# The maxima of the next head group spread over eleven slots of sixteen, and the long run of values three slots later

## The reference

```python
query = seq2 + b_self
key = concat([seq1 + b_prev, seq2 + b_self]); value = concat([seq1, seq2])
q, k, v = query @ Wq + bq, key @ Wk + bk, value @ Wv + bv      # split into 16 heads
score_prev = (q @ k_prev.T) * SCALE                            # masked past seq_len1
score_self = (q * k_self).sum(-1) * SCALE
weights = softmax(concat([score_prev, score_self]))
attn = weights[:-1] @ v_prev + weights[-1] * v_self
x = x + attn @ Wo + bo
h = gelu(x @ W1 + b1)
x = x + concat([h @ W2 + b2, h @ We[index] + be[index]])
```

## Time and profile before

| | |
|---|---|
| median of 3 runs | 1813.7 us (1807.92 to 1817.87) |
| profiled execution | 1807.68 us, span 1805.6 us |
| mean granted clock of TensorE | 0.975 of 2.4 GHz |
| busy | TensorE 1725.9 us (96%), weight loads 1266.5, VectorE 930.9, ScalarE 711.6, GpSimd 666.0 |
| first part | 32 groups, tiles of scores from 73.8 to 1005.7 us |
| length of a group in the middle | 25.2 to 38.2 us |

### The profile page before, as it was taken

One profiled execution on the slowest core, in us unless ns is written; L12 is line 12 of the kernel. 1 busy time (PEld: TensorE's weight loads), 2 busy tenths in 40 slices (PEclk: granted clock), 3 DMA queues, 4 the chain that ended last, 5 costly groups with the idle time before them and its releaser, 6 DMA issues.

```text
span 1805.6 us, 27964 instructions
## 1 busy us (share of the span) xinstructions
PE 1725.9 (96%) x8256; PEld 1266.5 (70%) x8256; DVE 930.9 (52%) x1430; ACT 711.6 (39%) x1259; POOL 666.0 (37%) x521
## 2 busy tenths in 40 slices
PE   6999999999999999999997899999999999999996
PEld 5666666657566566665662688888888888888885
DVE  4576576775766768657678633232232323232321
ACT  3254353544444435445445443323232323233322
POOL 3176575675774847657656301000010101010101
PEclk8999999999999999999997999999999999999998
DMA  6452435433534445253435432223141413232212
GB/s 143 76 115 62 108 80 115 92 77 82 111 93 88 92 88 117 52 109 83 97 82 150 115 115 50 68 49 85 46 87 41 87 52 78 59 66 70 47 30 53
DMA packets 370269, 149.45 MB, mean 83 GB/s; under 512 B 289226, under 2 KB 329162, under 8 KB 370194
## 3 DMA queue, kind: packets, MB, share of 16 engines
q1 hardware_dynamic: 364966, 146.28, 35.8%
q10 hardware_dynamic: 5228, 2.35, 0.5%
HBM read 70.41 MB, written 27.28 MB: 54 GB/s over the span
## 4 chain that ended last, share of the span: by engine, by line
PE 79%; issue 5%; DMA 4%; SPq 4%; DVE 4%; POOL 3%; ACT 1%; ACTq 0%; DVEq 0%; POOLq 0%
PE ps_proj L1258 15%; PE ps_av L1210 6%; PE ps_av L1212 6%; PE ps_av L1211 6%; PE ps_max L1289 6%; PE ps_av L1329 6%; PE ps_score L1316 5%; PE ps_proj L1210 3%; PE ps_proj L1211 3%; PE ps_proj L1212 3%; PE ps_max L1212 3%; PE ps_max L1211 3%; PE ps_max L1210 3%; DMA stacks<-parts 3%; PE ps_score L1212 3%
## 5 line engine op out<-in xcount | busy, mean ns | idle before, releaser
L729 ACT ACTIVATE p_f<-ps_score 128x512 f32<-128x512 f32 x512 | 304.0, 599 | 456.6 <-PE ps_score L1316 419.3
L941 DVE TENSOR_REDUCE m_col<-ps_max 128x1 f32<-128x512 f32 x512 | 328.7, 683 | 195.7 <-PE ps_max L1289 194.6
L604 POOL TENSOR_TENSOR p_sum<-p_sum,p_f 128x512 f32<-128x512 f32 x256 | 338.2, 1353 | 3.3 <-ACT p_f L729 3.3
L644 POOL TENSOR_TENSOR z_f<-z_f,a_raw 128x512 f32<-128x512 f32 x32 | 40.9, 1288 | 750.3 <-ACT z_f L842 726.0
L1135 DVE TENSOR_TENSOR h_lo<-h_f,h_hi 128x512 fp32r<-128x512 f32 x128 | 88.0, 688 | 411.8 <-ACT h_hi L833 411.7
L601 POOL TENSOR_TENSOR p_sum<-p_f 128x512 f32<-128x512 f32 x128 | 161.6, 1295 | 214.8 <-PE ps_av L1338 211.8
L1258 PE MATMUL ps_proj<-in_hi,w_hi 128*128 128x512 f32 x512 | 209.5, 409 | 14.4 <-POOL in_lo L609 11.1
L1289 PE MATMUL ps_max<-stacks 97*128 97x512 f32 x512 | 191.2, 438 | 29.7 <-DMA stacks<-parts 14.5
L1316 PE MATMUL ps_score<-stacks 99*128 99x512 f32 x512 | 209.2, 420 | 5.6 <-ACT p_f L729 5.4
L1258 PE MATMUL ps_proj<-in_lo,w_hi 128*128 128x512 f32 x512 | 207.1, 404 | 0.0
L1258 PE MATMUL ps_proj<-in_hi,w_lo 128*128 128x512 f32 x512 | 206.8, 404 | 0.0
(11 more groups left out here) (129 smaller groups left out, 2720.2 us busy)
## 6 DMA issues: line engine op xcount, KB each, us to landing
stacks<-parts SPq DMA_DIRECT2D x384, 128.0 KB
raw<-in_x_dram SPq DMA_DIRECT2D x128, 64.0 KB, 2.3
raw<-in_fside_BxSxS_dram SPq DMA_DIRECT2D x128, 64.0 KB, 2.2
den<-own_scratch SPq DMA_DIRECT2D x128, 64.0 KB, 2.8
attn_scratch<-num SPq DMA_DIRECT2D x32, 256.0 KB, 3.0
x_raw<-in_x_dram SPq DMA_DIRECT2D x128, 64.0 KB, 2.2
we_raw<-in_L_cond_We_dram SPq DMA_DIRECT2D x32, 256.0 KB, 2.8
resid_scratch<-a_raw SPq DMA_DIRECT2D x32, 256.0 KB, 2.0
```

The lines of the kernel that those rows point to most:

```text
L604: pool.tensor_tensor(p_sum[:, j], p_sum[:, j], now, ALU.add).then_inc(sum_made, 1)
L729: act.activation(p_f[:, i % FLIGHT], ps_score[i % 2][:, :], ACT.Exp, scale=SCALE).then_inc(p_made, 1)
L941: dve.tensor_reduce(m_col[:, n % C, n // C:n // C + 1], ps_max[n % 2][:, :], AX.X, ALU.max).then_inc(max_made, 1)
```

## The change

The tiles of maxima go into slots 0 to 10 (one or two in a slot) instead of 0 to 7 (two in a slot). The long run, with own scores and the turned maxima in it, goes from slot 8 to slot 11. The projection pieces of slots 9 to 11 go to slots 8 to 10; those behind the run are in slots 12, 13 and 14 or 15. ScalarE doubles the columns and copies the own scores ahead of slot 12 instead of 9, and sends its two blocks of `m_neg` after slot 13 instead of 11. VectorE makes `m_neg` in slot 12 instead of 9, and the denominator there too, behind it, instead of in slot 10. GpSimd's additions begin in slot 11 instead of 9 and end in slot 6 of the next group instead of 4; seven instead of five are left after the loop. SyncE's program is the same.

```diff
         def tiles_of_max(i):
 
-            ends = (2, 4, 6, 8, 10, 12, 14, TILES)
+            ends = (2, 3, 5, 6, 8, 9, 11, 12, 14, 15, TILES)
             return range(ends[i - 1] if i else 0, ends[i]) if i < len(ends) else range(0)
...
+        RUN = 11
+
         def thirds_of(g, i):
 
-            slots = ((4, 5, 5, 6, 7, 7, 9, 10, 11, 12, 13, 14), (0, 2, 3, 4, 5, 6, 9, 10, 11, 12, 13, 14),
-                     (0, 2, 3, 6, 7, 7, 9, 10, 11, 12, 13, 15), (0, 2, 3, 4, 5, 6, 9, 10, 11, 12, 13, 15))[g]
+            slots = ((4, 5, 5, 6, 7, 7, 8, 9, 10, 12, 13, 15), (0, 2, 3, 4, 5, 6, 8, 9, 10, 12, 13, 14),
+                     (0, 2, 3, 6, 7, 7, 8, 9, 10, 12, 13, 15), (0, 2, 3, 4, 5, 6, 8, 9, 10, 12, 13, 15))[g]
...
-                        n = (i + 7) % TILES
-                        if i >= 9:
+                        n = (i - RUN) % TILES
+                        if i >= RUN:
                             add_probabilities(b, g, 1 + n // HG, n % HG)
                         elif n < SUMS and not (first and g == 0):
                             add_probabilities(*after(b, g, -1), 1 + n // HG, n % HG)
 
             batches(pool, batch)
-            for n in range(7, SUMS):
+            for n in range(TILES - RUN, SUMS):
                 add_probabilities(B - 1, C - 1, 1 + n // HG, n % HG)
...
-                        if i == 9 and maximum:
+                        if i == RUN + 1 and maximum:
                             maxima_twice(*nxt)
                             own_row(*nxt)
                         if i == 15 and maximum:
                             own_weight(*nxt)
                         probabilities(b, g, i)
-                        if i == 11 and maximum:
+                        if i == RUN + 2 and maximum:
                             maxima(*nxt, range(2, C))
...
-                        if i == 10 and started:
-                            denominator(*after(b, g, -1))
...
-                        if i == 9 and bound:
+                        if i == RUN + 1 and bound:
                             own_max(*nxt)
                             m_parts(*nxt)
                             own_less_max(*nxt)
+                        if i == RUN + 1 and started:
+                            denominator(*after(b, g, -1))
...
-                        if i == 8:
+                        if i == RUN:
                             for t in (0, 1):
                                 value_burst(b, g, t)
                             if not (first and g == 0):
                                 denominators(*after(b, g, -1))
-                        if bound and i == 8:
+                        if bound and i == RUN:
                             own_scores(*nxt)
                             turn_max(*nxt)
```

## The result

Four executions of the changed kernel took 1905.1 us in the median (1899.0 to 1912.1), against 1814.2 of the kernel before (1807.9 to 1817.9): a ratio of 1.050, with an interval of 1.046 to 1.054. The profiled execution took 1904.4 us, its span 1902.3, which is 96.7 us longer than that of before.

A forecast was written before the change was run, and what follows sets the result against it. TensorE's own work, or short waits hidden by its busy share, was taken as the bound. 1807.7 + 35 (work) + 48 (clock) = 1891 us profiled, 1896 against the median; forecast 1878 to 1925 (0.58), range 1840 to 1925.

The forecast's parts named there:

- The chain in the tail: Behind the long run: transfers keep their length while TensorE's work falls to 3.8 us; four tails 28.5 us against 32.75.
- The price of the moved work: Fronts: 3.48 us more per group, 5.6 us of idle time saved per batch; with the tails, +4.1 us a batch.
- The clock: Behind the tails: falls to 1.2 GHz after four of five of 30 tails, 2.0 us each, +48 us.
- The strict reading of the Trainium skill: Gaps in the tails: only longer unbroken waits lower the clock, so it would stand and only +35 us remain.
- The last batch: Last batch: first two groups cost +3.3 us; seven sums left after the loop instead of five, +3 us.
- The first score after the run: Start of the tail: ready at 3.8 us, it waits for ScalarE's rows until 5.2 us after the long run.
- (1) The clock holds: Tails stall as worked out but 2.4 GHz is kept in nearly all; median 1849 us, 1835 to 1865; chance 0.28.
- (2) The chain hides: Tails: rows and first copy land by 4.05 us, when TensorE's work ends; faster, median 1748 us; chance 0.04.
- the turning point: Tails: the change turns faster from a tail of about 6.1 us on, needing 1 us less in the chain.
- (3) GpSimd becomes the bound: Two crowded groups: sums begin three slots later, probabilities wait 4 us more each batch; 1928 us; chance 0.05.
- probabilities that wait for sums: Sign of being wrong: a probability needs its buffer's sum eight or more slots later; such waiting was costed at nothing.
- (4) The fronts give back more: Fronts save more idle time, at whole clock: +1.6 us a batch, 1833 us or no change; chance 0.05.

The follow-up runs named there:

- the filled gap: Changed kernel with 11 matmuls nobody needs ahead of a group's first tile of maxima, in all batches but the last: 1865.6 us, ratio 1.028.
- the kernel with the old end: Changed kernel with groups 3 and 4 of the last batch in the schedule of before: 1899.7 us, ratio 1.047.
- copy first: Changed kernel with SyncE sending the first head's operand copy ahead of its two rows of `m_neg`: 1864.6 us, ratio 1.026.
- five pieces behind the run: Changed kernel with five projection pieces behind the run instead of three: 1833.1 us, ratio 1.012; with copy first as well, 1819.3 us, ratio 1.004.
- run at slot 9: Changed kernel with the long run at slot 9 instead of 11, maxima in nine slots, five pieces behind the run: 1839.7 us, ratio 1.013.

## Why the prediction was right, and where its terms were off

**The chain in the tail: shown.** The chain was read as fixed by SyncE's queue, with the copy behind the two rows, and it is: its links came at 1.37, 1.39, 3.11 and 8.06 us where 1.37, 1.40, 3.05 and 7.25 had been worked out, and turning two entries of that queue around took the tails to 5.4 to 6.4 us. The landing was mis-sized. In the tail shown, the copy was there 2.72 us after the end of its last issue (443.28), not 2.0 as before the change; the tails took 7.6 and 8.1 us in two groups, 7.25 in the other two. Together 30.2 instead of 28.5.

**The price of the moved work: shown.** 3.48 us a group was to go ahead of the run. At whole clock the changed kernel's fronts (those of the filled gap) are 31.59, 20.77, 21.13 and 20.65 us, 94.1 together against 92.8 worked out: 1.3 us less of the idle time was recovered than the 5.6 I had let it save. With the tails, 29.8 there, a batch at whole clock is 124.0 us, +6.7 against 117.24, not +4.1. The first 28 groups of the filled gap take 41.4 us more than before, where I had 29.

**The clock: shown, and near its size.** Falls behind 24 of 30 tails at 2.0 us had been taken, +48. There were 23, and the filled gap, which removes 20 of them, gives 39.5 us, 2.0 for each; in the shown batch they cost 1.6 to 2.1. By the traces of the first 28 groups it is 35.5 us, where my term was 45. The 81.9 us more at half speed (150.2 against 68.3) are no measure of the cost by themselves: half of a stretch at 1.2 GHz would have been needed anyway, and part of it lies in waits. The strict reading of the Trainium skill ("TensorE: Matmul & The Clock Gate", section "HAM oscillation — how this bites in real kernels"), by which only longer unbroken waits let the clock fall, is not borne out: here 0.54 us, one matmul, and 3.03 us were enough.

**The two errors offset each other.** The first 28 groups took 76.9 us more. My terms for seven batches were 29 for the work and 28/30 of 48, 45, for the clock: 74. The filled gap splits the measured time into 41.4 and 35.5. So the mechanism was right, but that the sum came out this close is in part luck: 12.4 us too little for the work and 9.5 too much for the clock.

**The last batch: too cheap.** I had 3.3 and 3 us, and about 3 of the clock's, some 10; it took 17.7. By the starts of its groups these are 4.7, 5.6, 3.9 and 3.6 us. The first two, for which I had 3.3, took 10.3, with 13.7 us at half speed where there was none before. The fourth I had at about its size, and the kernel with the old end gives 3.4 of it back, but for another reason than the sums that are left after the loop: before, the run stood in slot 8, in the 5.9 us between that slot's score (987.30) and the first output projection (993.16). Now 5.7 us pass there as well, 4.9 of them a wait for the projection's low parts, and the run's 2.7 us (1093.45 to 1096.16) come on top, in slot 11. That is read from the traces; it was not tried alone.

**Small terms.** The first score after the run was expected 5.2 us behind it and came at 4.5: ScalarE's issues ended at 3.18 and the rows were there 1.35 us later, not 2.0. This cost nothing, since the copy came last. The waits for low parts fell as expected (11.1 to 7.1 us), those for the reduces did not (10.1 to 11.3).

**The rivals.** (1) The clock holds, 1849: ruled out by the filled gap, whose 1865.6 us is where that rival would have been once the work's own terms are corrected. (2) The chain hides: ruled out by the tails; where I did make them short, VectorE's chain came next. I had put the turning point at a tail of about 6.1 us; with tails of 5.4 to 6.4 us (copy first) the kernel is still 2.6% slower, and with five pieces behind the run as well it is no faster than before. (3) GpSimd becomes the bound: ruled out. I had named probabilities that wait for sums as a sign of being wrong, and in the 32 groups they do wait more: ScalarE's waits for `p_sum` grew from 20.1 to 51.8 us. But TensorE's waits for probabilities did not grow (4.4 us, before 5.4), and the old order of the sums, which brings their place in the queue forward but not the run that they wait for, changes nothing. (4) The fronts give back more: they gave back 4.3 us in a batch, not 8.1.

**What stays open.** What decides whether a normalization inside a run of GpSimd's sums takes 1.5 or 7 to 9 us, and whether the sums are the cause; no experiment moved them apart. Without the stretched ones the steady batch of 116.4 us might be had in the whole program; no kernel that was run shows it.

## What to carry to other kernels

When a long piece of work starts a chain of small steps on other engines and queues, find the chain's length first, and then the work that stands over it: the tail here was 7.2 to 8.1 us whether some 21 or some 30 matmuls stood in it, and so each matmul taken from it was paid ahead of the run, less what looser maxima gave back there (4.3 us of 13.9 in a batch). The remedy was not to shorten the chain but to put independent pieces back over it (72 us for two pieces a group, the clock's share included); shortening it only uncovered the next one, VectorE's, which is 7.7 us long. Where work is moved and the waits don't fall, look at the longest case of the moved instruction, not at its mean: the normalization took 7.05 us in places, 2.5 on average. And a gap has two prices: its own length, and the slow clock of the work behind it, which here was 39.5 us of 91.

## What the runs showed of the hardware

The two landings differ: in the tail shown, the rows of `m_neg` were there 1.35 us after their last issue (441.12 to 442.47), the operand copy 2.72 us after its own (2.0 in the tail of before). I had given both 2.0.

Matmuls whose result nobody uses, 11 in each gap of some 3 us, kept the clock at 1.00 through the whole steady batch and made the kernel 39.5 us shorter; with two useful pieces in place of them, and 1.8 to 1.9 us of idle time left in one gap of a batch, a fall stood behind that gap in three batches (1.80 to 1.86 us) and none in two (1.77 and 1.87).

A VectorE instruction on two 128x512 tiles that takes 0.7 to 1.8 us in most groups took 6.6 to 9.0 us in some, each time inside an unbroken run of GpSimd's additions, and ended 0.54 or 0.55 us after it. The same instruction, begun 6.4 us into such a run, took 1.68 us in one group and 9.03 in another (run at slot 9).
